# One-head cross attention: no barrier behind five experts' tail, keys and values ahead of x, value bias added by GpSimd

## The chip, the cores and the metric

The kernel runs on one core of a Trainium2 chip. The metric is the device time of one execution in microseconds. A run before the change takes 1731.24 us (median of 3, 1727.58 to 1733.03).

## The reference

Four layers, each a cross attention and a feed-forward part, work on x of 4 x 512 x 128 with a context of 4 x 154 x 128. Each part is added to x behind a gate, tanh of a given number. The change is in the cross attention of layer 1 and at both its ends:

```python
x = x + tanh(g_ffn[0]) * moe(layernorm(x))          # layer 0: 8 experts, each token goes to its best one
# layer 1, cross attention, one head of width 128, no scale
q = layernorm(x) @ Wq.T + bq
k = ctx @ Wk.T + bk
v = ctx @ Wv.T + bv
x = x + tanh(g_xattn[1]) * (softmax(q @ k.T) @ v)
x = x + tanh(g_ffn[1]) * ffn(layernorm(x))          # layer 1: attention over the batch and 8 experts
```

Since the rows of the softmax sum to one, the bias bv comes out of the attention as it is.

## The kernel before, in words

x stays in SBUF as 16 tiles of 128 tokens; a batch is four tiles. The program has eight stages, two for each layer: 0 image, 1 experts, 2 onehead (this attention), 3 batch, 4 masked, 5 scaled, 6 decoder, 7 mixture. Each engine runs its own list of instructions in the order written, and waits on semaphores which the others raise. The order is written by hand; nothing plans it. There are eight PSUM banks; `bank` (L282) makes TensorE wait until the last reader of a bank is done. `barrier` (L379) makes an engine wait until the last batch of x of the stage before is done.

A layer norm is spread over engines. For batch b of stage s, `follow_measure` (L463) is VectorE's moments (L415, L418, L420), `follow_power` (L467) GpSimd's power to minus a half (L445), `follow_scale` (L470) VectorE's four scalings (L451), `follow_turn` (L490) TensorE's four transposes into bank 7 (L480), and `follow_turned` (L493) ScalarE's copy into xt (L486).

The tail of stage 1: GpSimd scatters the experts' rows to DRAM (`experts_po`, L1369), SP waits for all of them and reads the sums back batch by batch (L1393), and VectorE adds each to x (L1354). The norms of batches 0 to 2 follow in the tail, all sums and moments before the first scaling; batch 3 follows behind the barrier of stage 2.

Stage 2: TensorE makes keys (`onehead_pe`, L1433), the four queries (L1440) and the values (L1444). The bias of a query is added by VectorE (L1503) or ScalarE (L1476), VectorE copies the values (L1508, L1509). Then a loop over batches: scores (L1453), VectorE's maxima (L1515), ScalarE's exponentials with their sums (L1486), and `weigh`: transposes (L1414), copies by ScalarE (L1492) and VectorE (L1523), and the product with the values (L1423). `add_to_x` (L508) scales the result, adds the bias (L514), and adds gate times this to x (L516), tile by tile. GpSimd casts the low halves of weights: those of stage 7 in `onehead_po` (L1541), and in `batch_ahead_po` (L1899) a memset (L1901), small casts, four pieces for stage 3 and eleven for stage 5 (L1897). SP loads the weights of stages 5 and 6 behind the barrier (L387).

Of the kernel before, what the change touches and what calls it, by code (L numbers as in the profile page):

```python
# [9 lines left out]
ALU = mybir.AluOpType  # L10
# [8 lines left out]
P = 128  # L19
# [120 lines left out]
def constants():  # L140
# [38 lines left out]
    for part in range(3):  # L179
# [19 lines left out]
        "qkv_kept": "q_high", "product": "low_b", "x_based": "low_b", "shares": "ve", "weighted": "ve", "multiplied": "ve", "centred_x": "ve", "tokens": "filled", "four_times": "filled", "wo_low": "filled", "mixed_low": "low_b", "summed": "router_steps", "ranked": "routed",  # L199
# [34 lines left out]
class Kernel:  # L234
# [866 lines left out]
    def experts_memory(self):  # L1101
# [17 lines left out]
        self.logits1, self.key1 = (room[:, n * wide:(n + 1) * wide].rearrange("p (t n) -> p t n", t=ROUTED) for n in (0, 1))  # L1119
        self.top1, self.best1, self.number1 = (room[:, 2 * wide + n * ROUTED:2 * wide + (n + 1) * ROUTED] for n in range(3))  # L1120
# [121 lines left out]
    def experts_pe(self, pe):  # L1242
# [50 lines left out]
        for b in range(BATCH - 1):  # L1293
            self.follow_turn(pe, 1, b)

    def experts_ac(self, ac):
# [26 lines left out]
        for b in range(BATCH - 1):  # L1323
            self.follow_turned(ac, 1, b)

    def experts_ve(self, ve):
# [24 lines left out]
        for b in range(BATCH):  # L1351
            ve.wait_ge(*self.at(f"dma_x{b}", 32))
            rows = self.rows_of(b)
            ve.scalar_tensor_tensor(self.x[:, rows, :], self.added1[:, rows, :], self.gates[:, 4:5], self.x[:, rows, :], ALU.mult,  # L1354
                                    ALU.add).then_inc(self.mark("x1", b))
            if b < BATCH - 1:
                self.follow_measure(ve, 1, b)
        for b in range(BATCH - 1):
            self.follow_scale(ve, 1, b)

    def experts_po(self, po):
# [9 lines left out]
        for b in range(BATCH - 1):  # L1371
            self.follow_power(po, 1, b)
# [24 lines left out]
    def onehead_memory(self):  # L1397
        self.work_at = 0
        self.k2, self.q2, self.v2 = self.place(CTX_ROWS), self.place(TOKENS), self.place(2 * BATCH, P)
        self.probs2 = [self.place(QT, CTX) for _ in range(2)]  # L1400
        self.probs2_t = [self.place(2, SEQ) for _ in range(2)]
        self.neg2, self.total2, self.inv2 = ([self.place(QT) for _ in range(BATCH)] for _ in range(3))

    def onehead_pe(self, pe):
        w = self.w[2]
        parts = ((0, P), (1, CTX_REST))

        def weigh(b):
# [10 lines left out]
            if b == 0:  # L1419
                pe.wait_ge(*self.at("values2", BATCH - 1))  # L1420
# [6 lines left out]
        self.barrier(pe, 2)  # L1427
        pe.wait_ge(*self.at("dma_weights2", 16))
        pe.wait_ge(*self.at("context", 2))
        for half in (0, 1):  # L1430
            bank = self.bank(pe, 4 + half, "keyed2", half)
# [3 lines left out]
        for b in range(BATCH):  # L1435
            if b == BATCH - 1:
                self.follow_turn(pe, 1, b)
            self.columns(pe, 1, b)
            bank = self.bank(pe, b, ("queried2_a", "queried2_b")[b % 2], b)
            pe.matmul(bank, w["wq"], self.xt[:, self.cols_of(b)], start=True, stop=True).then_inc(self.mark("queries2", b))  # L1440
        for b in range(BATCH):
            bank = self.bank(pe, 4 + b % 2, "values2", b)
            for n, rows in parts:
                m = pe.matmul(bank[0:rows, n * P:(n + 1) * P], self.context[:, b, n * P:n * P + rows], w["wv"], start=True, stop=True)  # L1444
            m.then_inc(self.mark("valued2", b))
        for b in range(BATCH):
            for g in (0, 1):
                bank = self.bank(pe, 2 * (b % 2) + g, "exp2", b, 2 * g + 1)
                if g == 0:
                    pe.wait_ge(*self.at(("queried2_a", "queried2_b")[b % 2], b))  # L1450
                    pe.wait_ge(*self.at("keyed2", b // 2))
                for n in (0, 1):
                    m = pe.matmul(bank[:, n * CTX:(n + 1) * CTX], self.q2[:, (QT * b + 2 * g + n) * P:(QT * b + 2 * g + n + 1) * P],  # L1453
# [1707 lines left out]
```

## Time and profile before

| | us |
|---|---|
| median of 3 runs | 1731.24 |
| profiled execution, its own time | 1731.66 |
| span of the profiled execution | 1729.8 |
| TensorE busy (matmul) | 1411.2 |
| VectorE busy | 1155.3 |
| GpSimd busy | 816.1 |
| ScalarE busy | 765.9 |

The span runs from the first to the last instruction on the chip; the run's time has the little around it too. All times in the rows are counted from the span's start. Busy times overlap between engines, so what an instruction costs depends on whether the next one on another engine is waiting for it. The chain of waits follows the work that ended last back to its beginning and lists what was run or waited for at each time. The granted clock (PEclk) is 1.00 where TensorE has its full 2.4 GHz and 0.50 at 1.2 GHz.

### The profile page before, as it was taken

How to read it: one execution, taken by the hardware profiler on the slowest of the kernel's cores; microseconds unless marked ns; L12 is line 12 of the kernel's file. 1: busy time of each engine (PE TensorE's matmuls, PEld its weight loads, DVE VectorE, ACT ScalarE, POOL GpSimd, SP SyncE). 2: the span in 40 equal slices, each digit the busy share in tenths (PEclk: the TensorE clock that was granted, in tenths of full speed). 3: DMA queues.
4: the chain of work that ended last, by engine and by line, in shares of the span. 5: the costliest groups of instructions: out<-in, count | busy, mean ns of one | idle time of the engine just before them, and what ended most of it. 6: DMA issues, size and time to landing. Idle time of an engine off the chain costs nothing.

```text
span 1729.8 us, 36301 instructions
## 1 busy us (share of the span) xinstructions
PE 1411.2 (82%) x13436; PEld 972.1 (56%) x13597; DVE 1155.3 (67%) x3020; ACT 765.9 (44%) x1520; POOL 816.1 (47%) x1236
## 2 busy tenths in 40 slices
PE   3999999999999886846788799958974885758997
PEld 2777777777777675634566455523443332524555
DVE  4889788877767764544763777554457565687864
ACT  2777667766766652511234265533211552201111
POOL 3789889977766881561335733000001301134330
PEclk9999999999999997965889899989987896879998
DMA  7332231221121202330000000000000000000000
GB/s 268 89 95 86 86 95 48 51 51 43 47 55 46 61 22 73 96 116 1 1 1 1 12 5 2 1 1 1 1 1 1 1 1 1 1 1 1 7 7 13
DMA packets 35476, 64.27 MB, mean 37 GB/s; under 512 B 7535, under 2 KB 25042, under 8 KB 34147
## 3 DMA queue, kind: packets, MB, share of 16 engines
q1 hardware_dynamic: 33831, 59.82, 11.6%
q8 instruction: 111, 1.82, 0.4%
q0 software_dynamic: 1472, 2.12, 0.4%
q14 instruction: 62, 0.51, 0.1%
HBM read 30.64 MB, written 12.66 MB: 25 GB/s over the span
## 4 chain that ended last, share of the span: by engine, by line
PE 60%; DVE 21%; ACT 7%; issue 5%; POOL 4%; DMA 1%; another core or an unknown queue 0%; ACTq 0%; SPq 0%; DVEq 0%; POOLq 0%
PE banks L505 16%; PE banks L745 6%; PE banks L773 5%; PE banks L734 5%; PE banks L2145 4%; DVE xn L451 2%; PE banks L2131 2%; PE banks L480 2%; ACT work L932 2%; PE banks L2839 2%; PE banks L2098 1%; DVE norm_room L415 1%; PE banks L2782 1%; PE banks L1423 1%; DVE work L817 1%
## 5 line engine op out<-in xcount | busy, mean ns | idle before, releaser
L1040 POOL TENSOR_TENSOR work<-work 128x512 bf16<-128x512 f32 (+1 forms) x512 | 358.7, 723 | 74.8 <-ACT work L932 73.8
L817 DVE TENSOR_REDUCE work<-banks 128x1 f32<-128x666 f32 x256 | 216.5, 846 | 67.6 <-PE banks L734 65.0
L445 POOL TENSOR_TENSOR norm_room<-norm_room,minus_half 128x4 f32<-128x4 f32 x48 | 50.2, 1045 | 398.7 <-DVE norm_room L420 383.2
L939 ACT ACTIVATE work<-banks,work 128x666 f32<-128x666 f32 x256 | 208.2, 813 | 35.8 <-DVE work L817 28.9
L932 ACT ACTIVATE work<-banks 128x512 f32<-128x512 f32 x256 | 152.8, 597 | 143.7 <-PE banks L745 143.3
L505 PE MATMUL banks<-work,weights_b 128*128 128x512 bf16 (+1 forms) x830 | 159.2, 349 | 17.7 <-DVE work L2474 5.9
L734 PE MATMUL banks<-work 128*128 128x154 bf16 (+1 forms) x899 | 160.3, 295 | 14.0 <-DMA work<-work 7.1
L745 PE MATMUL banks<-const,work 128*128 128x128 f32 x1024 | 158.7, 278 | 15.4 <-ACT work L932 12.3
L734 PEld LDWEIGHTS banks<-work 128*128 128x128 bf16 x1024 | 95.7, 98 | 85.1 <-DMA work<-work 7.8
L773 PE MATMUL banks<-work 128*128 128x65 bf16 (+1 forms) x3840 | 136.5, 193 | 3.0 <-POOL work L1040 1.8
L480 PE MATMUL banks<-const,xn 128*128 128x128 f32 x176 | 38.8, 361 | 118.6 <-DVE xn L451 80.0
L505 PEld LDWEIGHTS banks<-work,weights_b 128*128 128x128 bf16 (+1 forms) x840 | 82.9, 101 | 90.0 <-issue 24.5
L773 PEld LDWEIGHTS banks<-work 128*128 128x128 bf16 x3840 | 129.1, 97 | 3.8 <-POOL work L1040 3.3
L745 PEld LDWEIGHTS banks<-const,work 128*128 128x128 f32 x1024 | 110.9, 141 | 35.4 <-issue 34.4
L486 ACT ACTIVATE xt<-banks 128x512 f32<-128x512 f32 x40 | 23.9, 597 | 228.4 <-PE banks L480 228.4
L2222 DVE TENSOR_REDUCE work<-banks 128x2 f32<-128x308 f32 x192 | 86.6, 473 | 52.8 <-PE banks L2103 27.3
L3049 POOL TENSOR_TENSOR work<-work 128x512 bf16<-128x512 f32 x64 | 67.5, 1060 | 101.1 <-DVE work L3002 101.0
L2201 ACT ACTIVATE work<-banks 128x256 f32<-128x256 f32 (+1 forms) x256 | 85.7, 382 | 57.3 <-PE banks L2134 34.5
L480 PEld LDWEIGHTS banks<-const,xn 128*128 128x128 f32 x176 | 26.1, 183 | 130.5 <-DVE xn L451 73.8
L825 DVE COPY work<-banks 128x128 f32<-128x128 f32 x256 | 73.5, 287 | 26.8 <-PE banks L754 14.9
L2131 PE MATMUL banks<-work 128*128 128x256 bf16 (+1 forms) x256 | 65.6, 292 | 14.6 <-ACT work L2193 11.6
L754 PE MATMUL banks<-const,work 128*128 128x128 f32 x256 | 70.0, 274 | 0.5 <-DVE scratch L1187 0.5
(441 smaller groups left out, 3214.6 us busy)
## 6 DMA issues: line engine op xcount, KB each, us to landing
work<-work SPq DMA_DIRECT2D x128, 166.5 KB, 2.7
sorted<-in_pads SPq DMA_DIRECT2D x10, 838.5 KB
weights_b<-in_weights SPq DMA_DIRECT2D x1, 4120.0 KB, 23.9
work<-scratch SPq DMA_DIRECT2D x64, 64.0 KB, 2.2
weights_b<-in_weights SPq DMA_DIRECT2D x1, 2824.0 KB, 9.5
weights_a<-in_weights SPq DMA_DIRECT2D x1, 2056.0 KB
weights_a<-in_weights SPq DMA_DIRECT2D x1, 2050.0 KB, 10.4
work<-work SPq DMA_DIRECT2D x32, 64.0 KB, 1.9
```

The source lines that it names most:

```text
L480: i = pe.transpose(ps[:, j * P:j * P + rows], src[0:rows, j, :], self.eye[0:rows, 0:rows])
L505: m = pe.matmul(out, left(a), right(b), start=start and n == 0, stop=stop and n == 2)
L734: m = pe.matmul(slot[:, a:z], lhs, k[:, h, part, a:z], start=part == 0, stop=part == 1)
L745: m = pe.transpose(ps[:, t * P:(t + 1) * P], prob[:, t * P:(t + 1) * P], self.eye)
L773: pe.matmul(self.out_heads[:, 2 * j + h, 0:width], parts[:, h, t, j * P:(j + 1) * P, of_probs], v[:, t, of_values, h, 0:width], start=(h, ...
L817: ve.tensor_reduce(self.neg_max[i % 4], self.slot[i % 2][:, 0:KEYS0], AX_X, ALU.max, negate=True).then_inc(self.mark("max"))
L932: ac.activation(self.probs_t[u % 2][:, h, 0:4, j * P:(j + 1) * P], self.bank_a.rearrange("p (t n) -> p t n", t=4), ACT.Copy).then_inc(self ...
L939: ac.activation(self.probs[i % 3], self.slot[i % 2][:, 0:KEYS0], ACT.Exp, bias=self.neg_max[i % 4]).then_inc(self.mark("exp"))
L1040: po.tensor_tensor(parts[:, :, :, 0], exact, parts[:, :, :, 1], ALU.subtract).then_inc(self.mark(event, i - 3))
L2131: m = pe.matmul(bank, left, a.q4[b % 2][:, g, cols], start=True, stop=s != 4)
L2201: ac.activation(out, self.bank_of(k, HALF)[0:rows_n, :], ACT.Exp).then_inc(self.mark("exp4", s, n))
L2222: ve.tensor_reduce(a.most[u % 2][:, c % 2, 2 * g:2 * g + 2], self.bank_of(n % 3, 2 * CTX).rearrange("p (h k) -> p h k", h=2), AX_X, ALU.ma ...
```

## The change

What it does, by engine:
- The barriers of stage 2 go. Stage 2's buffers now lie behind those of stage 1 in the work area instead of over them (`experts_end`).
- TensorE makes keys and values right after the experts' last transposes, in banks 0 and 1 and 2 to 5. Then the queries of batches 0 and 1, scores 0, query 2, scores 1, query 3, weigh 0, scores 2, weigh 1, and on. All queries and transposes use bank 7.
- ScalarE adds all query biases, and copies the values with the gate as scale.
- VectorE adds sum 0 to x and measures, then for each next batch: sum, scaling of the batch before, moments; the maxima of batch 0 stand before the moments of batch 3. Its part of `weigh` no longer comes behind the exponentials of the next batch. x takes one instruction per tile.
- GpSimd makes a row of gate times bias, casts stage 7's weights, and then runs the four powers; then it adds the row to each batch of x (`onehead_base_po`), after that batch's scaling. The eleven casts for stage 5 move to the end of the masked stage.
- SP loads the weights of stages 5 and 6 once the experts' last matmuls are through, behind the reads of the sums.

```diff
@@ experts_pe, experts_ac, experts_po: without follow_turn, follow_turned and follow_power of stage 1, batches 0 to 2
@@ experts_ve: the loops over BATCH at its end go; each batch's wait and sum become experts_x_ve(ve, b)
@@ onehead_memory
-        self.work_at = 0
+        self.work_at = self.experts_end
...
+        self.base2 = self.place(P)
@@ onehead_pe
+        def query(b):
+            self.follow_turn(pe, 1, b)
+            self.columns(pe, 1, b)
+            bank = self.bank(pe, 7, "queried2", b)
+            pe.matmul(bank, w["wq"], self.xt[:, self.cols_of(b)], start=True, stop=True).then_inc(self.mark("queries2", b))
+
+        def scores(b):
+            pe.wait_ge(*self.at("queried2", b))
+            pe.wait_ge(*self.at("keyed2", b // 2))
...
-        self.barrier(pe, 2)
         pe.wait_ge(*self.at("dma_weights2", 16))
         pe.wait_ge(*self.at("context", 2))
...
+            bank = self.bank(pe, 2 + b, "kept_v2", b)
             for n, rows in parts:
                 m = pe.matmul(bank[0:rows, n * P:(n + 1) * P], self.context[:, b, n * P:n * P + rows], w["wv"], start=True, stop=True)
             m.then_inc(self.mark("valued2", b))
+        query(0)
+        query(1)
         for b in range(BATCH):
+            scores(b)
+            if b + 2 < BATCH:
+                query(b + 2)
             if b > 0:
                 weigh(b - 1)
@@ onehead_ac
-        self.barrier(ac, 2)
+        def query(b):
+            self.follow_turned(ac, 1, b)
+            ac.wait_ge(*self.at("queries2", b))
+            ac.activation(self.q2[:, self.cols_of(b)], self.bank_of(7), ACT.Identity, bias=w["bq"]).then_inc(self.mark("queried2", b))
...
+            ac.activation(self.v2[:, 2 * b, :], bank[:, 0:P], ACT.Copy, scale=gate)
+            ac.activation(self.v2[0:CTX_REST, 2 * b + 1, :], bank[0:CTX_REST, P:2 * P], ACT.Copy,
+                          scale=gate[0:CTX_REST]).then_inc(self.mark("kept_v2", b))
+        query(0)
+        query(1)
...
+                if b + 2 < BATCH:
+                    query(b + 2)
@@ onehead_ve
-        self.barrier(ve, 2)
-        ve.wait_ge(*self.at("dma_weights2", 16))
-        self.follow_measure(ve, 1, BATCH - 1)
+        self.experts_x_ve(ve, 0)
+        self.follow_measure(ve, 1, 0)
+        for b in (1, 2, 3):
+            self.experts_x_ve(ve, b)
+            self.follow_scale(ve, 1, b - 1)
+            if b == 3:
+                most(0)
+            self.follow_measure(ve, 1, b)
         self.follow_scale(ve, 1, BATCH - 1)
...
+            ve.wait_ge(*self.at("x_based2", old))
+            for t in range(QT):
+                x = self.x[:, QT * old + t, :]
+                i = ve.scalar_tensor_tensor(x, self.bank_of(6)[:, t * P:(t + 1) * P], self.inv2[old][:, t:t + 1], x, ALU.mult, ALU.add)
+            i.then_inc(self.mark("x2", old))
@@ onehead_po
+    def onehead_base_po(self, po, b):
+
+        x = self.x[:, self.rows_of(b), :]
+        po.wait_ge(*self.at("normed", "follow", 1, b))
+        po.tensor_tensor(x, x, self.base2.unsqueeze(1).to_broadcast([P, QT, P]), ALU.add).then_inc(self.mark("x_based2", b))
 
     def onehead_po(self, po):
-        self.follow_power(po, 1, BATCH - 1)
+        po.wait_ge(*self.own("po", po.tensor_tensor(self.base2, self.row["L1_xattn_bv"], self.gates[:, 1:2].to_broadcast([P, P]), ALU.mult)))
...
+        for b in range(BATCH):
+            self.follow_power(po, 1, b)
+        for b in range(BATCH):
+            self.onehead_base_po(po, b)
         self.batch_ahead_po(po)
@@ onehead_sp
-        self.barrier(sp, 2)
+        sp.wait_ge(*self.at("shifted1", SORTED - 1))
         self.load_weights(sp, 5)
         self.load_weights(sp, 6)
@@ batch_ahead_po: its last lines become scaled_ahead_po, called at the end of context_po
+    def scaled_ahead_po(self, po):
         po.wait_ge(*self.at("dma_weights5", 16))
         for name, c in self.split5_chunks():
             self.batch_low_po(po, self.w[5][name][:, c * BANK:(c + 1) * BANK], "low5", name, c)
...
         if s == 4:
+            self.scaled_ahead_po(po)
             self.follow_power(po, 4, BATCH - 2)
```

## Rows read from the trace of the kernel before

**Rows 1.** Chain of waits, 715 to 835 us: start us, us, what
```profile
743.62 0.76 DVE x L1354
...
784.39 0.36 DVE scratch L514
...
785.12 0.27 DVE scratch L514
...
787.11 0.88 DVE norm_room L415 x4
...
789.07 1.60 ACT work L1486 x8
...
802.34 2.05 PE banks L1453 x8
804.39 1.72 PE banks L1414 x8
```

**Rows 2.** TensorE's timeline: start us, us, line, operation, tiles, count, idle before
```profile
752.00 1.12 PE L480 MATMUL banks<-const,xn 128*128 128x128 f32 x4 [17.61 <-DVE xn L451]
...
756.64 2.24 PE L1433 MATMUL banks<-context,weights_c 128*128 128x154 f32 x8
...
766.40 2.08 PE L1440 MATMUL banks<-xt,weights_c 128*128 128x512 f32 x2 [0.69 <-ACT xt L486]
768.27 5.03 PE L1444 MATMUL banks<-weights_c,context 128*128 128x128 f32 x16
...
791.59 5.83 PE L1423 MATMUL banks<-work 128*128 128x128 f32 x16 [3.18 <-DVE work L1523]
...
806.96 3.63 PE L1423 MATMUL banks<-work 128*128 128x128 f32 x16 [0.86 <-DVE work L1523]
```

**Rows 3.** GpSimd's timeline, 718 to 840 us, columns as in TensorE's
```profile
738.47 0.98 POOL L1369 DMA_INDIRECT added<-work  x1 [0.30 <-issue]
745.99 1.47 POOL L445 TENSOR_TENSOR norm_room<-norm_room,minus_half 128x4 f32<-128x4 f32 x1 [6.54 <-DVE norm_room L420]
...
756.44 6.03 POOL L1541 TENSOR_TENSOR weights_a<-weights_a 128x512 bf16<-128x512 f32 x6
762.41 0.95 POOL L1901 MEMSET split<- 128x1024 bf16 x1
...
771.01 11.02 POOL L1897 TENSOR_TENSOR weights_b<-weights_b 128x512 bf16<-128x512 f32 x11
...
839.68 1.27 POOL L1929 TENSOR_TENSOR x<-x,work 128x512 f32<-128x512 f32 x1
```

**Rows 4.** Windows: stretch, us, busy time and count per engine, PEclk, DMA share, GB/s
```profile
752.00:784.40 32.40, 24.20 (x89) 16.15 (x89) 12.12 (x39) 8.57 (x25) 25.98 (x30) 0.71 0.29 119
784.40:824.00 39.60, 27.00 (x96) 20.12 (x96) 17.80 (x69) 6.05 (x21) 3.04 (x3) 0.54 0.00 0
850.00:890.00 40.00, 31.14 (x196) 28.10 (x197) 30.79 (x71) 7.36 (x12) 7.96 (x8) 0.79 0.00 1
```

**Rows 5.** ScalarE's timeline, columns as in TensorE's
```profile
753.15 0.60 ACT L486 ACTIVATE xt<-banks 128x512 f32<-128x512 f32 x1 [19.89 <-PE banks L480]
...
768.52 0.69 ACT L1476 ACTIVATE work<-banks,weights_c 128x512 f32<-128x512 f32 x1 [2.17 <-PE banks L1440]
```

**Rows 6.** VectorE's timeline, 750 to 802 us
```profile
762.16 2.83 DVE L451 TENSOR_SCALAR xn<-x,norm_room 128x128 f32<-128x128 f32 x4
...
788.50 0.86 DVE L1515 TENSOR_REDUCE work<-banks 128x2 f32<-128x308 f32 x2
...
800.06 1.11 DVE L451 TENSOR_SCALAR xn<-x,norm_room 128x128 f32<-128x128 f32 x4
```

**Rows 7.** GpSimd's timeline, end of the masked stage
```profile
1074.69 1.48 POOL L2341 TENSOR_SCALAR work<-work 26x512 bf16<-26x512 uint8 x1
1105.82 1.03 POOL L445 TENSOR_TENSOR norm_room<-norm_room,minus_half 128x4 f32<-128x4 f32 x1 [29.65 <-DVE norm_room L420]
```

**Rows 8.** DMA issues, 700 to 800 us: tiles, queue, count, KB, us to landing
```profile
weights_b<-in_weights SPq DMA_DIRECT2D x1, 1027.5 KB, 12.2
```

More of the change, by code:

```diff
@@ L1292, in experts_pe @@
                 back(s - 3)
-        for b in range(BATCH - 1):
-            self.follow_turn(pe, 1, b)
     def experts_ac(self, ac):
@@ L1350, in experts_ve, with experts_x_ve @@
                 ve.tensor_copy(self.back1[o % 3], self.bank_of(7, SORT).rearrange("p (h d) -> p h d", h=2)).then_inc(self.mark("back1", o))
[L1351 to L1359, printed above, removed]
+    def experts_x_ve(self, ve, b):
+        ve.wait_ge(*self.at(f"dma_x{b}", 32))
+        rows = self.rows_of(b)
+        ve.scalar_tensor_tensor(self.x[:, rows, :], self.added1[:, rows, :], self.gates[:, 4:5], self.x[:, rows, :], ALU.mult,
+                                ALU.add).then_inc(self.mark("x1", b))
     def experts_po(self, po):
@@ L1406, in onehead_pe @@
         parts = ((0, P), (1, CTX_REST))
+        def query(b):
[6 more added lines that the diff above has]
+            pe.wait_ge(*self.at("keyed2", b // 2))
+            for g in (0, 1):
+                bank = self.bank(pe, 2 * (b % 2) + g, "exp2", b, 2 * g + 1)
+                for n in (0, 1):
+                    m = pe.matmul(bank[:, n * CTX:(n + 1) * CTX], self.q2[:, (QT * b + 2 * g + n) * P:(QT * b + 2 * g + n + 1) * P],
+                                  self.k2[:, b * CTX:(b + 1) * CTX], start=True, stop=True)
+                m.then_inc(self.mark("scores2", b, g))
         def weigh(b):
@@ L1430, in onehead_pe @@
         for half in (0, 1):
-            bank = self.bank(pe, 4 + half, "keyed2", half)
+            bank = self.bank(pe, half, "keyed2", half)
             for n in (0, 1):
@@ L1435, in onehead_pe @@
         for b in range(BATCH):
[L1436 to L1442, printed above, removed]
+            bank = self.bank(pe, 2 + b, "kept_v2", b)
             for n, rows in parts:
@@ L1445, in onehead_pe @@
             m.then_inc(self.mark("valued2", b))
+        query(0)
+        query(1)
         for b in range(BATCH):
[L1447 to L1453, printed above, removed]
-                                  self.k2[:, b * CTX:(b + 1) * CTX], start=True, stop=True)
-                m.then_inc(self.mark("scores2", b, g))
+            scores(b)
+            if b + 2 < BATCH:
+                query(b + 2)
             if b > 0:
```

71 lines of the change are left out of this document (27 added, 44 removed).

## The prediction, made before the changed kernel was run

> **What bounds the kernel now.** I first looked for the stage in the chain of waits. Its start is fixed by data: the first read of the experts' sums lands and VectorE adds it to x at 743.62 us. From there to the last batch of x the chain never leaves the attention, and it alternates short pieces of TensorE, ScalarE and VectorE [rows 1]: at 784.39 the first product of probabilities and values is scaled, at 802.34 and 804.39 scores and transposes run. No engine is full; the stage is a latency chain. The engine timelines show what fills it. TensorE stands idle 17.61 us before its first transposes at 752.00 [rows 2], although keys and values need nothing of x: the keys (2.24 us) run at 756.64 and the values (5.03 us) at 768.27, both inside the chain. GpSimd casts weights from 756.44 to 782 [rows 3], between norms of x that are short. The windows show TensorE's granted clock at a mean of 0.71 (752 to 784.4) and 0.54 (784.4 to 824) [rows 4]: mostly the lower of its two levels, 1.2 GHz. So a matmul here has two prices: the product with the values takes 3.63 or 5.83 us [rows 2].
>
> **Part 1, keys and values before x is there.** The barrier is gone, so TensorE makes them right after the experts' last transposes at about 734.4 (752.00 less the idle 17.61). At the lower clock they cost at most 2.24 + 5.03 = 7.3 us, done by 741.7; ScalarE's copies (two for keys, eight for values, each under the 0.69 us of a 128x512 one [rows 5]) end some 2 us later. The cover is the wait for the scattered rows and their re-read until 743.62; with it gone, the 7.3 us would be back on the chain. GpSimd now casts stage 7's weights first: its last scatter ends at 739.45, the new bias row (under 1 us) and six casts of 6.03 us [rows 3] take it to about 746. The first variance is ready when its power starts now, 745.99 [rows 3]. Cost of that: 0 to 0.5 us. The power in its way takes 1.47 us.
>
> **Part 2, sums, norms and scores by entry.** New order on VectorE: sum 0, moments 0, sum 1, scale 0, and so on. First power 745.99 + 1.47, plus 0.7 for port conflicts (below), plus one scale of 1.11 us (four pieces [rows 6]): the first transposes start at 749.3 instead of 752.0. Then, at the lower clock, with some 0.1 us at each hand-over:
> batch 0: transposes 1.12, copy 0.60, query 2.08, bias 0.69 [rows 2, 5]: to 754.2.
> batch 1 must follow, since transposes and query share bank 7: 1.12 + 0.60 + 2.08 and hand-overs: 758.3. Scores of batch 0, 2.05 [rows 1]: 760.3.
> batch 2: its transposes run while ScalarE makes the exponentials of batch 0. Two maxima take VectorE 0.86 [rows 6] and four exponentials with their sums ScalarE 1.60 [rows 1]; half of both, 1.2 to 1.3 us, comes after the last scores. Then copy 0.7 and query 2.08: 764.4. Scores of batch 1, 2.05: 766.5.
> batch 3 the same: 1.3 + 0.7 + 2.08: 770.6.
> Then weighing batch 0: transposes 1.72 [rows 1], VectorE's copy (as ScalarE's, 0.60 [rows 5]) and 0.15, product 5.83: 778.9 in all. Today the scaling after this product starts at 784.39, so 5.5 us are won if every matmul runs at 1.2 GHz.
> TensorE's own share of that chain is 2 x 1.12 + 4 x 2.08 + 2 x 2.05 + 1.72 + 5.83 = 22.2 us. At 2.4 GHz the product is 2.2 us shorter, a query about 1 us (half of 2.08), the rest together about 3: some 9 us less, ending at 770. Which level is granted I cannot derive, so I take today's mix: a mean of 0.71 between 0.5 and 1.0 is 42% of the time at full. 0.42 x 9 = 3.8: product 0 ends at 775.1, **9.3 us earlier**.
>
> **Part 3, value bias by GpSimd.** Today each batch of x takes eight dependent VectorE pieces, 784.39 to 787.11, where the moments begin: 2.7 us. A piece with a PSUM input takes 0.36, or 0.27 of the chain behind another [rows 1]. Four of them and the end of the last: 1.2 us. The values already hold the gate, for nothing: ScalarE's copies replace VectorE's. This lies on the chain in all four batches: 4 x 1.48 = **5.9 us**. GpSimd pays four base adds; one of this shape takes 1.27 us [rows 3], all four follow the fourth power at about 763 and end near 768, before x of batch 0 is due at 775. If they were late, each would cost its 1.27. The memset and casts ahead of stage 3 come behind them and take about 8.6 us (762.41 to 771.01 now [rows 3]), to 777; the first power of stage 2 is due at about 778. That is a cover of 1 us only; uncovered it would cost up to 1 or 2.
>
> **Part 4, what is moved.** Eleven casts (11.02 us [rows 3]) go from here to the end of the masked stage on GpSimd. There GpSimd idles 29.65 us before the power at 1105.82, its previous work ending at 1076.2 [rows 7]: they end at 1087, and stage 5, which needs them, begins after that power. Zero, with 18 us to spare. SP asks for the weights of stages 5 and 6 after the four reads of the sums rather than after the last sum; the second had landed 12.2 us after its issue [rows 8] and in the new order nothing waits for it before 1076. Zero, unless it slows those reads (rival).
>
> **Two losses.** Clock: today one of the three later products runs at 3.63. With the mean at 0.54 that is luck that a shift can lose; bounds 0 and 2.2, I take 1.1. Ports: VectorE's scaling of batch 3 took 2.83 instead of 1.11 us beside the memset that GpSimd starts at 762.41 [rows 3, 6]. In the new order that scaling meets the base adds: at most 3 x 1.27 = 3.8, with about 2 us of slack until batch 3's transposes; bounds 0 and 1.8, I take 0.5.
> The Trainium skill, "SBUF — State Buffer", section "Who interferes with whom", says VectorE and GpSimd share one port pair under an exclusive lock, and that a VectorE instruction with two SBUF inputs is blocked by a GpSimd one that reads SBUF. The slow scaling agrees; by the page the sums of x too would wait for whole casts.
>
> **Sum**: 9.3 + 5.9 - 1.1 - 0.5 = 13.6 us. The profiled execution took 1731.66 us (span 1729.8 and 1.9 around it), 0.4 over the median of 1731.24; I subtract from the median: **1717.6 us**. All later stages follow x, so I let the gain pass through whole. It is well over the 5.2 us (0.3%) that a measurement of this kernel can tell from no change.
>
> **Rivals.**
> (A) TensorE stays at 1.2 GHz all through: 5.5 + 5.9 - 2.2 - 1.8 = 7.4, so 1723.8. For it: the mean of 0.54 in the second half. 0.15.
> (B) Keys and values out of the way leave queries and scores dense from 755 on, and the clock is full to product 0 and beyond: 9.3 becomes 14.3, 2.2 more on each of products 1 and 3: 24.6, so 1706.6. Against it: idle stretches of today's kind remain in each batch. 0.12.
> (C) The lock bites fully: the sums of x beside the six casts wait 1.04 twice (1.4 more than the 0.7 counted) and the scaling of batch 3 1.3 more: 1720.3. For it: [rows 3, 6]. Against it: the sum at 743.62 took its 0.76 [rows 1], though beside no large cast. (The Trainium skill's page on SBUF, cited above, has this as its rule.) 0.06.
> (D) The reads of the sums of batches 1 to 3 are mixed with the weights behind them: the weights are then asked for at about 743, and all land when they do, 12.2 us later [rows 8], at about 755; VectorE wants the second at 746 today: 9 us lost, 1726.6. Against it: the reads are issued first on the same queue. 0.03.
> (E) The barrier goes but the stage starts no earlier, because another wait (a bank, a semaphore counted in another order) holds TensorE: the values and keys stay in the chain and only what part 3 wins is left, less part of it: 1727 to 1731. 0.02.
> (F) Slower: the shift lands the next stage's products at half clock. Place: 850 to 890, where TensorE is busy 31 us at a mean of 0.79 [rows 4], so about 18 us of them at full. If all those ran at half, 18 us would be lost: 1735.6. It decides only when over 13.6 us of full-clock work turns to half. 0.02.
>
> **Numbers.** The forecast has 0.60. Faster: forecast, A, B, C: 0.93. Within: D and E: 0.05. Slower: F: 0.02. The range must hold 0.8: the forecast's own spread, C, most of A and the near half of B: 1709.0 to 1724.0. Outside are B's far end, D, E and F.
>
> **What the profile of the changed kernel would show.** Keys and values between 734 and 743; the six casts before the first power, and that power at 746 to 747; first transposes near 749.3; product 0 ending near 775; four VectorE pieces of 0.35 per batch of x and a distance of three batches shorter by 1.5 each; stage 3 beginning 12 to 15 us earlier; GpSimd's eleven casts from 1076 to 1087, and stages 3 to 7 as long as now. I am wrong if the second read of sums lands after 750, if the first power waits for casts beyond 747.5, if x of batch 0 waits for its base add, or if any later stage changes its length by over 3 us.

## The result, and the profile after

The changed kernel takes 1725.01 us (median of 20 runs, 1718.08 to 1733.10) against 1731.57 for the kernel before (20 runs, 1723.33 to 1737.79). The ratio is 0.9955, 95% interval 0.9944 to 0.9967: **0.45% or about 7.8 us faster**. The forecast was faster, by 13.6 us. 1725.0 lies 1.0 us above the range; set against 1731.24, the median that the forecast started from, the ratio gives 1723.5, just inside it. The profiled execution has a span of 1725.6 us, where the one of before had 1729.8. The program prints its lines under new numbers: the moved sum of x is L1352, queries L1405, scores L1413, products L1432, maxima L1510, the addition to x L1536, the base adds L1547.

TensorE's timeline of the changed kernel, columns as in [rows 2], which it answers:
```profile
734.09 1.21 PE L1441 MATMUL banks<-context,weights_c 128*128 128x154 f32 x8
735.14 2.96 PE L1446 MATMUL banks<-weights_c,context 128*128 128x128 f32 x16
750.23 1.12 PE L480 MATMUL banks<-const,xn 128*128 128x128 f32 x4 [12.14 <-DVE xn L451]
752.13 2.05 PE L1405 MATMUL banks<-xt,weights_c 128*128 128x512 f32 x2 [0.78 <-ACT xt L486]
...
763.04 1.10 PE L1405 MATMUL banks<-xt,weights_c 128*128 128x512 f32 x2 [1.18 <-ACT xt L486]
...
767.56 0.66 PE L480 MATMUL banks<-const,xn 128*128 128x128 f32 x4 [2.38 <-DVE xn L451]
770.14 2.05 PE L1405 MATMUL banks<-xt,weights_c 128*128 128x512 f32 x2 [1.93 <-ACT xt L486]
771.98 1.91 PE L1423 MATMUL banks<-const,work 128*128 128x128 f32 x8
774.87 5.83 PE L1432 MATMUL banks<-work 128*128 128x128 f32 x16 [0.97 <-DVE work L1528]
...
786.04 5.83 PE L1432 MATMUL banks<-work 128*128 128x128 f32 x16 [1.28 <-ACT work L1500]
...
799.85 3.68 PE L1432 MATMUL banks<-work 128*128 128x128 f32 x16 [0.86 <-DVE work L1528]
...
809.45 5.83 PE L1432 MATMUL banks<-work 128*128 128x128 f32 x16 [0.86 <-DVE work L1528]
```
Keys and values are gone from the chain: they run at 734 to 738, and the 17.61 us of idle time ahead of the first transposes have become 12.14. But product 0 runs at 774.87 for 5.83 us, wholly at the lower clock, and in front of it the transposes of batch 3 (767.56) waited 2.38 us for VectorE. In the kernel before, product 0 had part of the full clock:
```profile
780.29 4.06 PE L1423 MATMUL banks<-work 128*128 128x128 f32 x16 [2.09 <-DVE work L1523]
```

GpSimd's timeline, answering [rows 3]:
```profile
740.97 6.47 POOL L1555 TENSOR_TENSOR weights_a<-weights_a 128x512 bf16<-128x512 f32 x6
747.55 1.47 POOL L445 TENSOR_TENSOR norm_room<-norm_room,minus_half 128x4 f32<-128x4 f32 x1
...
763.98 3.18 POOL L1547 TENSOR_TENSOR x<-x,work 128x512 f32<-128x512 f32 x3
767.58 1.09 POOL L1547 TENSOR_TENSOR x<-x,work 128x512 f32<-128x512 f32 x1 [0.42 <-DVE xn L451]
...
773.22 4.04 POOL L1915 TENSOR_TENSOR weights_c<-weights_c 128x512 bf16<-128x512 f32 x4
783.47 1.03 POOL L445 TENSOR_TENSOR norm_room<-norm_room,minus_half 128x4 f32<-128x4 f32 x1 [6.21 <-DVE norm_room L420]
```
VectorE's, answering [rows 6]:
```profile
747.38 0.74 DVE L1352 SCALAR_TENSOR_TENSOR x<-work,gates,x 128x512 f32<-128x512 f32 x1
...
764.04 3.46 DVE L451 TENSOR_SCALAR xn<-x,norm_room 128x128 f32<-128x128 f32 x4 [1.12 <-POOL norm_room L445]
767.42 0.85 DVE L1510 TENSOR_REDUCE work<-banks 128x2 f32<-128x308 f32 x2
...
780.74 1.13 DVE L1536 SCALAR_TENSOR_TENSOR x<-banks,work,x 128x128 f32<-128x128 f32 x4 [6.04 <-PE banks L1432]
```
and the answer for that scaling alone, one tile's instructions with the shortest, middle and longest duration in ns:
```profile
L451 DVE TENSOR_SCALAR xn<-x,norm_room x4: 335/1116/1127, 764.0 to 767.2; 128x128 f32<-128x128 f32 x4
```
The scaling of batch 3 starts 0.06 us after the first base add, and three of its four pieces last about as long as one base add each (3.18 / 3 = 1.06 us); the fourth, between the third and the fourth base add, takes 0.34. The windows, as in [rows 4] (product 0 ended at 780.70 instead of 784.35; the third is the same stretch of the next stage; the last is the mixture stage):
```profile
750.20:780.70 30.50, 21.59 (x65) 13.37 (x65) 13.46 (x47) 8.80 (x25) 16.14 (x19) 0.61 0.19 81
780.70:816.40 35.70, 27.08 (x96) 20.21 (x96) 14.60 (x62) 6.06 (x21) 3.05 (x3) 0.55 0.00 1
839.00:880.00 41.00, 31.80 (x198) 28.53 (x200) 31.37 (x72) 7.75 (x12) 8.46 (x8) 0.79 0.00 1
1519.40:1725.60 206.20, 179.43 (x984) 102.15 (x997) 137.18 (x295) 31.39 (x87) 71.34 (x68) 0.90 0.02 6
```
and that last stage in the kernel before:
```profile
1531.80:1729.80 198.00, 170.69 (x984) 98.23 (x997) 137.18 (x295) 31.40 (x87) 71.33 (x68) 0.94 0.02 6
```
So the time came and went in two places. From the first sum of x (743.62, now 744.71) to the last x of the attention it was 83.0 us and is 71.7: **11.3 us won**. The mixture stage, whose instructions the change does not touch, took 198.0 us and takes 206.2: **8.2 us lost**. VectorE, ScalarE and GpSimd do there what they did, to 0.02 us; TensorE is busy 8.7 us longer at a mean clock of 0.90 instead of 0.94. The start of the stage came 1.1 us later and the stages between took 2.2 us less, so 4.2 us of span are left.

Two questions follow: why 11.3 instead of 13.6 in the stage, and whether the 8.2 belong to the change.

### The profile page after: what moved, and what is told of

Same layout as the page of the kernel before. It is cut to its first block, busy times and chain, and to the rows that moved or that the text cites. A ratio compares the mean times of both kernels' runs of the same rounds, so it can differ in the third digit from the quotient of the medians.

```text
span 1725.6 us, 36290 instructions
## 1 busy us (share of the span) xinstructions
PE 1421.8 (82%) x13436; PEld 977.8 (57%) x13597; DVE 1149.3 (67%) x2994; ACT 769.5 (45%) x1530; POOL 821.9 (48%) x1241
## 4 chain that ended last, share of the span: by engine, by line
PE 60%; DVE 20%; issue 7%; ACT 6%; POOL 4%; DMA 2%; SPq 0%; another core or an unknown queue 0%; ACTq 0%; DVEq 0%; POOLq 0%
PE banks L505 15%; PE banks L745 6%; PE banks L773 5%; PE banks L734 5%; PE banks L2165 4%; DVE xn L451 2%; PE banks L2151 2%; PE banks L480 2%; ACT work L932 2%; PE banks L2860 2%; PE banks L2118 1%; PE banks L2803 1%; PE banks L1432 1%; DVE norm_room L415 1%; POOL work L1040 1%
## 5 line engine op out<-in xcount | busy, mean ns | idle before, releaser
L734 PE MATMUL banks<-work 128*128 128x154 bf16 (+1 forms) x899 | 161.8, 297 | 13.6 <-DMA work<-work 7.0
L505 PEld LDWEIGHTS banks<-work,weights_b 128*128 128x128 bf16 (+1 forms) x840 | 83.1, 101 | 89.7 <-issue 24.7
L486 ACT ACTIVATE xt<-banks 128x512 f32<-128x512 f32 x40 | 23.9, 597 | 207.5 <-PE banks L480 207.5
L2151 PE MATMUL banks<-work 128*128 128x256 bf16 (+1 forms) x256 | 65.7, 292 | 14.2 <-ACT work L2213 11.6
```

Of the source, the lines that this page charges most:

```text
L505: m = pe.matmul(out, left(a), right(b), start=start and n == 0, stop=stop and n == 2)
L734: m = pe.matmul(slot[:, a:z], lhs, k[:, h, part, a:z], start=part == 0, stop=part == 1)
L2151: m = pe.matmul(bank, left, a.q4[b % 2][:, g, cols], start=True, stop=s != 4)
```

## The experiments

Lengths in the table are read from the timelines: from the first sum of x to the last addition to x in the attention (in brackets: first sum to the end of product 0), and the mixture stage, from its first VectorE instruction to the end. "Half" is the time in such a stretch in which the granted clock was 0.5. Totals are device times: the median where a ratio with its interval stands beside it, else the one execution. The lengths always come from one profiled execution, whose own time can differ from the median (base_late 1712.52, warm2 1718.88, late_low5 1718.43, late_warm 1703.84, bias_undone 1723.83). The clock of 0.5 is 1.2 GHz.

| kernel | attention | half | mixture | half | total | ratio to before |
|---|---|---|---|---|---|---|
| before, first profile | 83.0 (40.7) | 66.0 | 198.0 | 23.9 | 1731.66 | |
| rep_before | 83.1 (40.5) | 62.6 | 204.5 | 37.2 | 1730.96 | |
| after, first profile | 71.7 (36.0) | 61.5 | 206.2 | 42.4 | 1727.45 | |
| rep_after | 71.5 (36.0) | 61.3 | 206.2 | 42.4 | 1721.59 | |
| base_late | 64.3 (28.9) | 43.8 | 206.2 | 42.4 | 1710.84 | 0.9879 [0.9864, 0.9894] |
| bias_undone | 77.6 (34.3) | 63.9 | 206.2 | 42.4 | 1726.87 | 0.9969 [0.9958, 0.9980] |
| kv_late | 81.2 (43.3) | 74.4 | 206.2 | 42.4 | 1728.49 | |
| low5_back | 72.9 (36.0) | 62.7 | 197.9 | 23.8 | 1715.44 | |
| warm2 | 68.4 (34.3) | 43.1 | 204.5 | 37.2 | 1718.55 | 0.9923 [0.9899, 0.9946] |
| best | 62.0 (27.7) | 41.5 | 197.9 | 23.8 | 1705.14 | 0.9863 [0.9836, 0.9890] |
| late_low5 | 71.0 (30.5) | 57.4 | 206.2 | 42.4 | 1716.65 | 0.9912 [0.9893, 0.9931] |
| shift_a | 68.4 (32.7) | 58.2 | 207.2 | 43.4 | 1719.25 | |
| shift_b | 64.3 (28.9) | 43.8 | 203.6 | 32.9 | 1709.96 | |
| late_warm | 63.8 (28.0) | 32.9 | 197.9 | 23.9 | 1705.75 | 0.9868 [0.9841, 0.9895] |

**Both kernels once more.** No edit.

> The kernel before, once more, for its clock. Theory 1 (luck of the clock in stage 7): the free 2.4 GHz of the first profile in stage 7 (16.9 us at half from 1537 us to the end) is not tied to this kernel; a second execution shows another amount, and stage 7 is longer by about 0.45 us for each further us at half. Theory 2 (the change itself shifts stage 7): the amount is again about 17 us, and the last batch of x in the attention is again near 826.6 us, the length from the first sum of x to there 83.0 us within 3 us.

> The changed kernel, once more. Theory 1 (luck of the clock): stage 7 shows another amount at half clock than the 35.7 us of its first profile, in either direction, and everything else keeps its length. Theory 2 (tied to the change): again 33 to 38 us at half and again 8 us longer than the first profile of before. Both: from the first sum of x to the end of the last one in the attention 71.7 us within 3 us.

The gain within the stage repeats (83.1 to 71.5, 11.6 us). The mixture stage of the kernel before took 204.5 us this time, of the changed one 206.2 again; the spans differ by 9.4 us (1729.2 and 1719.8). So a good part of the 8.2 us was the one execution of before that the first profile caught. Its total was an ordinary one all the same: the first sum of x came at 743.62, in rep_before at 737.92.

**base_late: is VectorE's scaling held by the base adds, and does it matter?**
```diff
+        po.wait_ge(*self.at("normed", "follow", 1, BATCH - 1))
         for b in range(BATCH):
             self.onehead_base_po(po, b)
```

> GpSimd waits for the scaling of batch 3 before its four base adds. Theory lock: that scaling falls from 3.46 us to 1.1 us, the transposes of batch 3 start up to 2.3 us earlier, and x of the attention ends 1.5 to 2.3 us earlier; the base adds end near 769.5 and no batch of x waits for them. Theory slack: the scaling is shorter, but TensorE and ScalarE are late anyway (exponentials of batch 1), and the end moves by less than 0.5 us.

The chain had no room for the stall: the attention is 7.2 us shorter than in rep_after, where the theory of the lock had at most 2.3, and the ratio to the kernel before is 0.9879 instead of 0.9955. The two ratios lie some 13 us apart; the attention shows 7.2 of them, and where the others come from is not shown. TensorE's timeline of base_late:
```profile
758.54 0.64 PE L480 MATMUL banks<-const,xn 128*128 128x128 f32 x4
761.12 1.10 PE L1405 MATMUL banks<-xt,weights_c 128*128 128x512 f32 x2 [1.93 <-ACT xt L486]
762.05 1.04 PE L1423 MATMUL banks<-const,work 128*128 128x128 f32 x8
764.06 3.37 PE L1432 MATMUL banks<-work 128*128 128x128 f32 x16 [0.97 <-DVE work L1528]
```
and its VectorE and GpSimd:
```profile
757.36 1.11 DVE L451 TENSOR_SCALAR xn<-x,norm_room 128x128 f32<-128x128 f32 x4 [1.12 <-POOL norm_room L445]
```
```profile
758.55 4.23 POOL L1547 TENSOR_TENSOR x<-x,work 128x512 f32<-128x512 f32 x4 [1.23 <-DVE xn L451]
```
The scaling is back at 1.11 us, the transposes of batch 3 wait for nothing, and product 0 runs at full clock. 7.2 us is three times the stall of 2.35. The rest is clock, which shift_a below happens to separate.

**shift_a and shift_b: is the mixture stage's length fixed by its instructions?** Both are base_late with copies that nothing needs (3 and 8) ahead of the first scaling of the mixture stage:
```diff
+                if n == 0:
+                    for _ in range(3):
+                        ve.wait_ge(*self.own("ve", ve.tensor_copy(self.scratch[:, 0:4, :], self.x[:, 0:4, :])))
```

> base_late with three dependent VectorE copies (128x512, into a free tile) before the first scaling of the mixture stage, that is some 1.5 us of delay there and nothing else. Theory 1 (the half-clock stretches of the mixture stage sit at fixed places relative to the work ahead of it; a shift of the stage against them changes which matmuls meet them): the stage's length jumps to another of 198, 204.5 and 206.2 plus the delay, so the total moves by something other than +1.5: about 1704 or 1710. Theory 2 (the order of instructions inside the stage alone fixes its length): total 1710.8 + 1.5 = 1712.3 and 42 us of half clock in the stage as in base_late.

> As shift_a with eight copies, some 4 to 5 us of delay before the first scaling of the mixture stage. Theory 1 (which matmuls meet half-clock stretches depends on the shift): half clock in the stage is not 42 us but near 24 or 37, and the total is 1707 to 1709 or stays near 1714. Theory 2 (order of instructions alone): total 1715 to 1716, half clock in the stage 42 us.

The windows of the mixture stage, shift_b:
```profile
1504.50:1708.10 203.60, 174.73 (x999) 99.07 (x997) 140.75 (x303) 31.39 (x87) 71.33 (x68) 0.92 0.02 6
```
and base_late:
```profile
1504.40:1710.70 206.30, 181.12 (x999) 102.06 (x997) 137.14 (x295) 31.40 (x87) 71.31 (x68) 0.90 0.02 6
```
Up to 1504.4 the two executions agree to 0.1 us in every stage. Then shift_b does eight copies more (VectorE's count is 303 instead of 295, 3.6 us) and is done 2.6 us **sooner**: TensorE is busy 6.4 us less, with 32.9 us at half clock instead of 42.4. So the stage's length is not fixed by its instructions, as the kernel before had shown without any edit (198.0 and 204.5). That the copies did it, by moving the matmuls against the stretches at half clock, is not shown: each is one execution, and base_late itself was timed from 1710.52 to 1712.52, its shortest 0.6 us above shift_b's 1709.96. In shift_a the stage took 1.0 us more, with 43.4 us at half clock, near theory 2; its total met neither theory, because of the attention.

Shift_a shows a second thing. Its program up to the mixture stage is base_late's, yet its attention took 68.4 us:
```profile
752.77 2.26 PE L1413 MATMUL banks<-work 128*128 128x154 f32 x8
...
761.84 1.10 PE L1405 MATMUL banks<-xt,weights_c 128*128 128x512 f32 x2 [1.94 <-ACT xt L486]
762.77 1.87 PE L1423 MATMUL banks<-const,work 128*128 128x128 f32 x8
765.61 5.83 PE L1432 MATMUL banks<-work 128*128 128x128 f32 x16 [0.97 <-DVE work L1528]
```
The scaling took 1.12 us and was not held, but product 0 ran at half clock. So with product 0 at half clock on both sides the base adds' stall costs 71.5 - 68.4 = 3.1 us of attention: 2.35 for the scaling itself and 0.95 because the query of batch 3, which comes earlier without the stall, is still at full clock (1.10 us instead of 2.05), less 0.2 behind product 0. The clock on the same instructions makes another 68.4 - 64.3 = 4.1. The Trainium skill's page "TensorE: Matmul & The Clock Gate" says in its Part 1, on the clock gate, that one kernel shows different numbers of slow matmuls from execution to execution; base_late's instructions did.

**bias_undone: part 3 alone undone** (values without the gate, eight VectorE pieces per batch of x, no base adds).
```diff
-            ac.activation(self.v2[:, 2 * b, :], bank[:, 0:P], ACT.Copy, scale=gate)
+            ac.activation(self.v2[:, 2 * b, :], bank[:, 0:P], ACT.Copy)
...
-                i = ve.scalar_tensor_tensor(x, self.bank_of(6)[:, t * P:(t + 1) * P], self.inv2[old][:, t:t + 1], x, ALU.mult, ALU.add)
+                i = self.add_to_x(ve, QT * old + t, self.bank_of(6)[:, t * P:(t + 1) * P], 1, self.row["L1_xattn_bv"],
+                                  factor=self.inv2[old][:, t:t + 1])
...
-        for b in range(BATCH):
-            self.onehead_base_po(po, b)
```

> Part 3 alone is undone: values without the gate, the bias and the gate by VectorE in eight pieces per batch, no base adds. Theory of the sum: each x takes 2.7 us again instead of 1.13, four times on the chain, so plus 6.2 us, less 2.3 us that the base adds' lock no longer costs: x ends 3.5 to 4.5 us later than in the changed kernel. Rival (the bias was hidden): less than 2 us.

The attention is 6.1 us longer than in rep_after, more than the 3.5 to 4.5 expected. Product 0 ends 1.7 us earlier (34.3 for 36.0), and from there to the end the stage takes 43.3 instead of 35.5 us. The 1.7 us are clock (product 0 takes 4.29 us instead of 5.83), not the missing base adds: the scaling of batch 3 now meets GpSimd's memset and small casts and takes 2.49 us, and the first sum of x, which starts beside the six casts, takes 2.33 instead of 0.89. Of the 7.8 us behind product 0, 6.2 are four times the longer x; the rest is clock again (product 1 takes 4.98 us instead of 5.83, product 2 5.83 instead of 3.45). In VectorE's timeline of bias_undone a batch of x is again eight pieces, from 770.69 to 773.4, where the moments follow:
```profile
736.37 2.33 DVE L1352 SCALAR_TENSOR_TENSOR x<-work,gates,x 128x512 f32<-128x512 f32 x1 [9.16 <-DMA work<-added]
...
756.78 2.49 DVE L451 TENSOR_SCALAR xn<-x,norm_room 128x128 f32<-128x128 f32 x4 [1.12 <-POOL norm_room L445]
...
770.69 0.35 DVE L514 SCALAR_TENSOR_TENSOR scratch<-banks,work,rows 128x128 f32<-128x128 f32 x1 [4.50 <-PE banks L1432]
...
773.41 0.87 DVE L415 BATCH_NORM_STATS2 norm_room<-x 128x6 f32<-128x128 f32 x4
```
2.72 us against 1.16 (780.74 to 781.90 in the changed kernel), 1.56 a batch.

**kv_late: part 1 alone undone** (keys and values wait until batch 0 is normed).
```diff
         pe.wait_ge(*self.at("context", 2))
+        pe.wait_ge(*self.at("normed", "follow", 1, 0))
```

> Part 1 alone is undone: TensorE makes keys and values only once batch 0 of x is scaled, so 16 + 8 instructions (up to 2.24 + 5.03 us at half clock) lie in front of the first transposes again. Theory of the sum: from the first sum of x to the end of x in the attention 71.5 becomes 77 to 79 us. Rival (the clock gives it back): the extra dense matmuls raise the clock for the queries behind them, the time at half falls, and the stage grows by less than 4 us.

TensorE's timeline of kv_late:
```profile
743.38 2.39 PE L1442 MATMUL banks<-context,weights_c 128*128 128x154 f32 x8 [15.34 <-DVE xn L451]
745.56 5.04 PE L1447 MATMUL banks<-weights_c,context 128*128 128x128 f32 x16
750.52 1.11 PE L480 MATMUL banks<-const,xn 128*128 128x128 f32 x4
```
The first transposes come 12.9 us after the first sum instead of 5.6: 7.3 us. The attention is 9.7 us longer, over the 77 to 79 us expected; the other 2.4 is product 2, 5.83 us instead of 3.45. Dense work ahead of the chain bought no clock for it: product 0 takes 5.83 in both.

**low5_back and late_low5: part 4's move of eleven casts undone**, in the changed kernel and in base_late.
```diff
-    def scaled_ahead_po(self, po):
...
-            self.scaled_ahead_po(po)
```

> Part 4 alone is undone: the eleven casts for stage 5 (11.0 us) stand again behind those for stage 3. They then end near 282 us behind nothing but at about 44 us after the first sum of x, when the first variance of the next norm has been ready for 5 us; the scaling that needs it stands behind x of batch 1, some 3 us later still. Theory: GpSimd's powers wait, nobody else does, and the stage keeps 71.5 us within 1. Rival: VectorE's copies and sums meet the casts at the shared port and the stage grows by 2 to 4 us.

> base_late with part 4's casts of stage 5 put back (the eleven GpSimd casts run at the end of the experts again instead of at the end of the masked stage). Theory 1 (which of its discrete lengths the mixture stage takes goes with the order of the work ahead of it, not with when it is reached): the mixture stage takes 198 us instead of base_late's 206.2, the attention 64.3 + 1.4 = 65.7 us, total 1710.8 + 1.4 - 8.2 + about 1 = 1704 to 1706. Theory 2 (the length is luck of the arrival time or of the execution): the mixture stage keeps 206.2 or takes 204.5, total 1711 to 1713.

GpSimd's timeline of late_low5:
```profile
771.37 11.01 POOL L1916 TENSOR_TENSOR weights_b<-weights_b 128x512 bf16<-128x512 f32 x11
782.34 1.03 POOL L445 TENSOR_TENSOR norm_room<-norm_room,minus_half 128x4 f32<-128x4 f32 x1
```
With the casts back, the first power of the next norm, ready at 771.4, waits until 782.34, where base_late's starts at 771.32. In low5_back that costs the attention 1.4 us, a little over the 1 us expected, in late_low5 6.7: 1.6 of it by the end of product 0, before the casts can matter (clock alone, the query of batch 2 took 2.05 us instead of 1.10), and 5.1 behind it, where x is ready earlier than in low5_back and waits the longer, and products 1 and 2 take 5.83 us instead of 4.94 and 4.24 (2.5 of the 5.1). So part 4 is worth nothing at the pace of the kernel before, where these casts end at 782 and the next power starts at 788.68; it is worth 1.4 us at that of the changed kernel, and more at that of base_late. The total of low5_back is nevertheless 6.15 us under rep_after, because its mixture stage took 197.9 us. Before late_low5 ran I held that this length follows the order of the casts; it kept 206.2 with the same order, so that theory fell. The short length came in four kernels, before (198.0), low5_back, best and late_warm (197.9), whose casts stand in different places.

**warm2 and late_warm: can TensorE be kept at full clock by work that nothing needs?** 48 and 2 dummy matmuls into a free bank, in the changed kernel and in base_late.
```diff
+        def filler(n):
+            ones = self.cb["ones"]
+            for _ in range(n):
+                pe.matmul(self.bank_of(6), ones, self.cb["spread1"][:, 0:BANK], start=True, stop=True)
...
+        filler(48)
         query(0)
+        filler(2)
         query(1)
```

> The changed kernel with 48 matmuls of 128x512 bf16 (0.21 us each) on an unused bank behind the values, while TensorE waits for x, and 2 more before the transposes of batch 1. Their results are read by nobody. Theory clock: the first transposes and queries run at 2.4 GHz (0.56 and 0.86 us instead of 1.12 and 2.05), product 0 ends 3 to 6 us earlier after the first sum, and the stage falls from 71.5 to 64 to 69 us. Rival (the lock and the hand-overs set the length): product 0 ends within 1.5 us of the 36.0 us it takes after the first sum now, clock or not.

> base_late plus the filler of warm2 (48 and 2 dummy matmuls of bf16 into a bank that is free, while TensorE waits for x and for the first query). Theory 1 (the two losses, half clock at the stage's start and VectorE's scaling held behind GpSimd, are separate and add up): the attention takes 64.3 - 3.1 = 61.2 us or less, total about 1707 if the later stages keep base_late's lengths. Theory 2 (base_late has already won the clock back from the middle of the stage on, so the filler gives only what the first products before it lost): 63 to 64 us, total 1709.5 to 1711.

TensorE's timeline of warm2:
```profile
732.58 10.31 PE L1439 MATMUL banks<-const_b 128*128 128x512 bf16 x47 [0.16 <-issue]
743.73 0.66 PE L480 MATMUL banks<-const,xn 128*128 128x128 f32 x4 [0.84 <-DVE xn L451]
745.16 1.10 PE L1405 MATMUL banks<-xt,weights_c 128*128 128x512 f32 x2 [0.78 <-ACT xt L486]
...
761.93 2.05 PE L1405 MATMUL banks<-xt,weights_c 128*128 128x512 f32 x2 [1.94 <-ACT xt L486]
763.77 1.91 PE L1423 MATMUL banks<-const,work 128*128 128x128 f32 x8
766.65 5.83 PE L1432 MATMUL banks<-work 128*128 128x128 f32 x16 [0.97 <-DVE work L1535]
```
The first transposes and query run at full clock (0.66 and 1.10 instead of 1.12 and 2.05), but the query of batch 1 takes 1.51 already, and behind the stall of batch 3 the clock is low again and product 0 takes 5.83. The stage wins 3.1 us, 1.7 of them by product 0. In late_warm the filler adds only 0.5 us to base_late's attention: the two remedies do not add up, as theory 2 had it. The mixture stage in its trace took 197.9 us, 8.3 less than base_late's.

**best: what the readings add up to.** base_late, the queries in bank 6 instead of the transposes' bank 7, the moments of batch 3 ahead of the maxima of batch 0, and the mixture stage's six casts behind the second power of the next stage's norm.
```diff
-            bank = self.bank(pe, 7, "queried2", b)
+            bank = self.bank(pe, 6, "queried2", b)
...
-            if b == 3:
-                most(0)
             self.follow_measure(ve, 1, b)
+            if b == 3:
+                most(0)
...
```

> On top of base_late: queries get bank 6, so transposes of the next batch need not wait for the bias of the last; the moments of batch 3 stand before the maxima of batch 0 (they fit the 1.7 us in which VectorE waits for scores); the six casts for stage 7 stand behind the second power of stage 2's norm instead of in front of the first of stage 1's. Expected from rows: 0.4 us for the first power, 0.8 us for the transposes of batch 1, up to 1.4 us for the scaling of batch 3: stage 64.3 becomes 62 to 63.5 us. Rival (clock): another phase of the clock loses or wins more than these 2 us together, anything from 59 to 68 us.

The attention takes 62.0 us, and the kernel 0.9863 of before: some 23.7 us won where the change had won 7.8. What each of the three additions is worth was not run by itself, and the intervals of best and base_late overlap.

## Why the prediction was right and wrong

The direction was right, and the size was 7.8 us where 13.6 was forecast. In the attention product 0 was to end 9.3 - 0.5 = 8.8 us earlier after the first sum and ended 4.7 earlier (40.7 to 36.0); behind it 4.8 us were to be won and 6.6 were: 11.3 in all. The rest of the difference arises outside the attention.

**Part 1 holds.** Keys and values end at 738.1, ScalarE's copies by 743.1, and nothing waits for them. Undone, they cost 7.3 us, the 7.3 of the text. The six casts ended at 747.44, the power started at 747.55, 2.84 us after the first sum instead of 2.37: the 0.5 that the text had as its upper bound. The 0.7 for port conflicts in part 2 had no row behind it; those 0.5 are all that the trace shows up to the first transposes.

**Part 2 was right in its order and wrong in its clock.** First transposes 5.5 us after the first sum, 5.7 predicted; all of the chain at half clock gave product 0 ending 35.3 us after the sum. I then took 3.8 us off, because the mean clock of today was 0.71, and came to 31.5; measured are 36.0. The clock was full on the query of batch 2, the scores of batch 1 and the transposes of batch 3 only (1.10, 1.21 and 0.66 us), where the saving ran into the wait for batch 3's scaling, and half on product 0, which [rows 2] shows at 5.83 for others and which the kernel before had in 4.06 (780.29 to 784.35). A mean clock over a stretch says nothing about which matmuls get it. Executions of the same order without the stall gave 28.9 (twice), 30.5 and 32.7 us, on both sides of the forecast's 31.5. So taking the mean was a guess that could have come out; it is not a working of the clock.

**The ports loss is the term that failed: 0.5 taken, 1.8 its upper bound, 3.1 measured** (rep_after to shift_a), and 7.2 with what the clock did in base_late. The step was "with about 2 us of slack until batch 3's transposes". That slack fits a schedule with every matmul at half clock, as the text's is; with the query of batch 2 and the scores of batch 1 at full clock they ended at 765.2 and TensorE stood waiting from then to 767.56. I had deducted the clock's gain in one sentence and kept the half clock's slack in another. In shift_a, without the stall, the scores of batch 1 end at 759.21 and the scaling at 759.19: no slack at all. The maxima of batch 1 stand behind the scaling on VectorE and the exponentials behind them, so these are held up with it; the 1.93 us until ScalarE has copied batch 3's transposes are not part of the price, since base_late has them too. The Trainium skill, "SBUF — State Buffer", section "Who interferes with whom", says that VectorE's scaling can take the pair that it shares with GpSimd and that whoever issues first holds it for a whole instruction. The trace agrees: three pieces of 1.12 us beside three adds of 1.06. Of rival C the scaling came about, larger than priced: 2.35 us. Its other half, sums of x held by the six casts, did not come in the changed kernel: the first sum took 0.83 us instead of 0.76, and the casts 6.47 instead of 6.03; the second, at 747.38, found the casts all but done (0.74). But it can come: in bias_undone the first sum took 2.33 us beside the same casts.

**Part 3 holds**: 1.56 us a batch measured, 1.48 predicted. From product 0 to the end the stage went from 42.3 to 35.7 us, 6.6 us, where 5.9 - 1.1 = 4.8 was forecast: the clock loss of 1.1 did not come (products 1 to 3 took 5.83, 3.68 and 5.83, as before). The base adds took 1.06 us each, not 1.27, and no x waited for them.

**Part 4**: the eleven casts ended at 1076.2 (a start of 1065.07 and 11.09 us), 18.5 us before the power at 1094.63, as forecast with 18. The casts kept ahead of stage 3 left 6.2 us of cover, not 1. That leaving the eleven there would have cost 1.4 us or more, the text did not count.

**"I let the gain pass through whole" is the second term that did not hold, and its cause is open.** The attention won 11.3 and 11.6 us in two pairs of traces; the ratio over 20 runs says 7.8, with 5.7 to 9.7 as its interval. So some 2 to 6 us less than the attention won arrive at the end. Where a trace shows time lost in stages that the change does not touch, it is TensorE at half clock in other places: 198.0, 203.6, 204.5, 206.2 and 207.2 us for one mixture stage. Rival F had this mechanism at 850 to 890, where nothing happened (a mean of 0.79 before and after); in the first pair of traces it came at 1520 and later. My own sign that I am wrong, a later stage changed by over 3 us, was met there, though the kernel before moved by 6.5 us there by itself.

Rival A (an all-half chain, 1723.8) came nearest in time, for nearly its reason: product 0 at 36.0, with most matmuls at half. D and E are refuted: the sums of x follow one another without waiting for data, and the first transposes moved. B's full clock from the queries on came in no trace of the changed kernel; product 0 itself was at full clock (3.37 us) in base_late, shift_b, late_low5 and best, all with the stall gone, behind first queries at half.

**What stays open.** How often each length of the mixture stage occurs in the 40 timed executions of the two kernels: total times of one kernel spread over 14 to 15 us, but only 14 executions in all have traces. The mean clock of the 20 executions of the changed kernel is on record, though, and it goes with the time: the fastest (1718.08) ran at 0.917 and the slowest (1733.10) at 0.902, and over the 20 the correlation of the time with the time at half clock is 0.91. So most of the spread is clock. The same figures give no sign that the change puts more half clock into the other stages: on average 310 us of half clock in the 20 executions, against 314 in 27 of the kernel before, with 61 against 64 in the attention. So the 3.6 us between the attention's gain and the ratio are a difference of many executions and two pairs of traces, and what makes them up is not shown. The other stages move from trace to trace too: the first sum of x came at 743.62 and 744.71 in the first two profiles and between 736.4 and 739.0 in the twelve others, and the stages between the attention and the mixture stage took 701.3 to 706.0 us.

Why the instructions of base_late met the full clock at product 0 in three traces (base_late, shift_b and late_low5) and not in a fourth (shift_a), I can't say; base_late's four timed executions lie within 2.0 us (1710.52 to 1712.52), and shift_a at 1719.25 is outside. Best and late_warm are ahead partly by mixture stages of 197.9; their longest timed executions were 1714.46 and 1714.04.

## What to carry to other kernels

When GpSimd work is put "beside" a chain, look at what VectorE does in the same microseconds and let that finish first: one wait of GpSimd's made the attention 7.2 us shorter here, 3.1 of them by the stall and the others by clock. Slack and clock must be worked out with one assumption: what makes TensorE faster takes away the cover that a stall elsewhere was hidden in. And of a gain of 10 us in one stage, check the untouched stages before it is credited or debited: judge a stage by its own length in the trace, and the kernel by many executions.

## What the runs showed of the hardware that I had not expected

- One untouched stage took 198.0 and 204.5 us in two executions of the same kernel, with 23.9 and 37.2 us at half clock, and with eight extra copies (3.6 us of VectorE) on its path it took 2.6 us less than without them (shift_b against base_late, one execution each; that the copies made it is not shown).
- The same instructions took 64.3 and 68.4 us in two executions (base_late, shift_a), product 0 3.37 and 5.83, with the first sum of x at 738.55 and 738.71; that the arrival made it is not shown.
- A 128x128 scaling of VectorE (0.34 us free) and a 128x512 add of GpSimd took turns, instruction by instruction, for three rounds; the adds were not slowed (1.06 each, and 4.23 for four in base_late), the scaling took 3.46 instead of 1.11.
- Which side waits is not always the same: the first sum of x beside the same six casts took 0.83 us in the changed kernel, and the casts 6.47 instead of 6.03; in bias_undone the sum took 2.33 and the casts 6.02. What decides it is not shown.
- Ten microseconds of dense dummy matmuls up to 0.84 us before the first transposes set the clock high for these and the first query, and it did not last: by product 0, after waits of 2.37 and 1.94 us, it was low as without them.
